# Two gated blocks in float32 on one core: second products of the units issued one half tick later, split inputs and products given more buffers, routing work moved

## The reference, cut to what matters

```python
scores = softmax(xt @ gate_w.T)
_, idx = top_k(scores + gate_bias, 2)
for e in range(8):
    gate_e = sum(where(idx == e, weights, 0.0), axis=1)
    h = silu(xt @ w1[e].T) * (xt @ w3[e].T)
    y = y + gate_e[:, None] * (h @ w2[e].T)
z = silu(xt @ sw1.T) * (xt @ sw3.T) @ sw2.T          # two shared units
return y + z
```

## Time and profile before

| what | value |
|---|---|
| median of three runs | 1388.08 us |
| profiled execution, its own time | 1374.39 us |
| span of its instructions | 1372.6 us |
| TensorE matmuls busy | 1122.3 us (82%) |
| VectorE busy | 1026.4 us (75%) |
| GpSimd busy | 637.2 us (46%) |
| ScalarE busy | 587.4 us (43%) |
| mean granted TensorE clock | 0.92 |

### The profile page before, as it was taken

The page is one execution under the profiler, slowest core; times in us unless marked ns, Lnnn a source line. Parts: engine busy times, 40 slices in busy tenths (PEclk is TensorE's granted clock), DMA queues, the critical chain, the costliest instruction groups (busy, mean ns, idle before and its releaser), DMA issues.

```text
span 1372.6 us, 23593 instructions
## 1 busy us (share of the span) xinstructions
PE 1122.3 (82%) x7464; PEld 961.7 (70%) x7464; DVE 1026.4 (75%) x2393; ACT 587.4 (43%) x1506; POOL 637.2 (46%) x377
## 2 busy tenths in 40 slices
PE   4244446999879996997989999998888888988887
PEld 2133324888768985886878989887777767777776
DVE  2999999989999999985364444447777777777766
ACT  2211212656446553654536454543334443443332
POOL 4889989898789979893301101011111111111000
PEclk9965555999979997999899999999999999999999
DMA  6101114988478965895561555510000000000000
GB/s 214 46 24 38 38 47 155 276 277 255 151 231 281 280 216 171 258 296 180 183 199 53 180 167 184 164 30 21 18 24 24 21 19 24 24 24 24 8 8 16
DMA packets 125036, 166.41 MB, mean 121 GB/s; under 512 B 10033, under 2 KB 67569, under 8 KB 124913
## 3 DMA queue, kind: packets, MB, share of 16 engines
q1 hardware_dynamic: 119792, 152.31, 35.9%
q0 software_dynamic: 5120, 12.59, 2.8%
HBM read 137.60 MB, written 27.26 MB: 120 GB/s over the span
## 4 chain that ended last, share of the span: by engine, by line
PE 55%; DVE 24%; issue 8%; POOL 6%; ACT 3%; SPq 2%; DMA 1%; DVEq 0%; POOLq 0%; ACTq 0%
PE ZB L1274 9%; PE YB L1288 6%; PE YD L1325 4%; DVE q_sb L896 4%; PE ZD L1242 3%; PE ZD L1244 3%; PE ZD L1243 3%; DVE s L871 3%; POOL prod L585 3%; PE ZD L1288 2%; PE YB L1325 2%; DVE hu L1094 2%; PE MC L1238 2%; POOL xs L595 2%; PE MA L1233 2%
## 5 line engine op out<-in xcount | busy, mean ns | idle before, releaser
L561 POOL TENSOR_TENSOR rstd<-ve,neghalf 128x4 f32<-128x4 f32 x64 | 65.7, 1026 | 581.3 <-DVE ve L825 580.9
L682 ACT ACTIVATE hid<-ZB,w2b 128x128 f32<-128x128 f32 x768 | 215.6, 377 | 163.5 <-PE YB L1288 81.5
L573 POOL TENSOR_TENSOR prod<-q_sb,kv_sb 128x2048 f32<-128x2048 f32 x48 | 216.3, 4508 | 53.4 <-DVE q_sb L896 33.3
L585 POOL TENSOR_TENSOR prod<-s,kv_sb 128x2048 f32<-128x2048 f32 x48 | 215.3, 4507 | 7.5 <-DVE q_sb L896 7.5
L1274 PE MATMUL ZB<-bt,w1b 128*128 128x128 f32 x1536 | 212.5, 284 | 1.2 <-ACT hid L682 0.9
L1274 PEld LDWEIGHTS ZB<-bt,w1b 128*128 128x128 f32 x1536 | 196.7, 200 | 4.0 <-issue 3.4
L704 ACT ACTIVATE own_prod<-ZD 128x512 f32<-128x512 f32 x102 | 61.1, 599 | 232.5 <-PE ZD L1244 230.9
L1288 PE MATMUL YB<-w2b,hid 128*128 128x128 f32 x1024 | 141.0, 281 | 0.0
L1288 PEld LDWEIGHTS YB<-w2b,hid 128*128 128x128 f32 x1024 | 128.5, 194 | 14.7 <-ACT hid L682 9.0
L1094 DVE TENSOR_TENSOR hu<-own_prod,ZD 128x512 f32<-128x512 f32 x102 | 69.8, 684 | 72.8 <-ACT own_prod L704 45.4
L1109 DVE SCALAR_TENSOR_TENSOR own_prod<-YD,gate,own_prod 128x128 f32<-128x128 f32 x320 | 89.9, 343 | 30.4 <-PE YD L1325 27.8
(11 more groups left out here) (250 smaller groups left out, 2335.0 us busy)
## 6 DMA issues: line engine op xcount, KB each, us to landing
w2b<-in_w SPq DMA_DIRECT2D x96, 516.0 KB
w1b<-in_w SPq DMA_DIRECT2D x96, 512.0 KB, 4.9
xb<-xs SPq DMA_DIRECT2D x96, 128.0 KB, 3.4
ctx_t<-in_ctx SPq DMA_DIRECT2D x32, 256.0 KB, 2.9
x2d<-x2s SPq DMA_DIRECT2D x48, 128.0 KB, 5.2
x<-in_x SPq DMA_DIRECT2D x16, 256.0 KB, 3.8
xs<-zrow SPq DMA_DIRECT2D x4, 1024.0 KB, 10.6
xrow<-in_x SPq DMA_DIRECT2D x16, 256.0 KB, 3.9
```

The costliest lines, as they stand in the source:

```text
L573: pool.tensor_tensor(out=prod[:, t % 2, :].rearrange("p (h e d) -> p h e d", h=HEADS, e=HEADS), in0=q.unsqueeze(2).broadcast_to([P, HEADS, ...
L585: pool.tensor_tensor(out=prod[:, (t + 1) % 2, :].rearrange("p (h d e) -> p h d e", h=HEADS, e=HEADS), in0=s0[:, t, :, :].unsqueeze(2).broa ...
L682: act.activation(hid[n % 2][:, j, k * RT:(k + 1) * RT], ZB[j // 2][:, at:at + RT], ACT.Relu, bias=w2b[t % 3][:, k, e, FJ * D + j:FJ * D + ...
```

## The change

The second products stand three halves after the first. `hu` gets three buffers, which lie in `prod`, a tile of the attention stage (the weight conversion, which borrowed hu, borrows vk_t and lk_t). ut_hi and ut_lo get two buffers each. The third norm moves half a tick to a tick earlier on GpSimd (kc 7 to kc 6) and a half earlier on ScalarE. ut_lo moves from h15 to h0 on VectorE, the product lg from h0 to h2 on TensorE (behind vk), logits_max from h0 to h3, score_parts from h6 to h5, route_tokens from h4 (behind hu2) to h6. No instruction of computation or transfer is added or taken away.

```diff
-UNIT_OUT = {pos + 2: u for pos, u in UNIT_IN.items()}
+UNIT_OUT = {pos + 3: u for pos, u in UNIT_IN.items()}
@@ bank_uses
-        if not later:
-            order += [(None, "lg", d) for d, k in d_parts(tick) if k == 0]
         stages = C_LATER if later else C_FIRST
         order += [(None, stages[k], c) for c, k in c_parts(tick) if k in stages]
+        if not later:
+            order += [(None, "lg", d) for d, k in d_parts(tick) if k == 1]
@@ buffers
-        ut_hi, ut_lo = sb("ut_hi", [P, CH], F32R), sb("ut_lo", [P, CH], F32R)
-        su, hu = own_prod[:, CH:3 * CH].rearrange("p (i n) -> p i n", i=2), sb("hu", [P, 2, CH])
+        ut_hi, ut_lo = ([sb(f"{n}{i}", [P, CH], F32R)[:] for i in range(2)] for n in ("ut_hi", "ut_lo"))
+        su = own_prod[:, CH:3 * CH].rearrange("p (i n) -> p i n", i=2)
+        hu = [prod[:, 0, i * CH:(i + 1) * CH] for i in range(1, 4)]
-        raw = [hu[:, i, :] for i in range(2)]
+        raw = [vk_t[:], lk_t[:]]
@@ GpSimd
-                        if kc == 7:
+                        if kc == 6:
                             norm(3, c)
@@ ScalarE, first half of a tick
+                        if kc == 7:
+                            if has(c - 1):
+                                filled(act, "xt3", c - 1)
+                            normed(3, lambda j: xn3[:, j, :], lambda j: x3[:, j, :], c)
@@ ScalarE, second half of a tick
                         if kc == 7:
-                            if has(c - 1):
-                                filled(act, "xt3", c - 1)
-                            normed(3, lambda j: xn3[:, j, :], lambda j: x3[:, j, :], c)
                             b = filled(act, "xt3", c)
-                            if has(c - 1):
-                                act.wait_ge(pe_gate.sem, pe_gate.at(c - 1))
-                            act.activation(ut_hi[:], b[:], ACT.Copy).then_inc(ut_hi_s.sem, 1)
+                            if has(c - 2):
+                                act.wait_ge(pe_gate.sem, pe_gate.at(c - 2))
+                            act.activation(ut_hi[c % 2], b[:], ACT.Copy).then_inc(ut_hi_s.sem, 1)
@@ VectorE, unit_gated
-                if u >= 2:
-                    dve.wait_ge(pe_f.sem, pe_f.at(d, max(1, u - 2)))
-                elif has(d - 1):
-                    dve.wait_ge(pe_f.sem, pe_f.at(d - 1, E1 + u))
-                dve.tensor_tensor(out=hu[:, u % 2, :], ...
+                old = d * UNITS + u - 3
+                if old >= 0:
+                    dve.wait_ge(pe_f.sem, pe_f.at(old // UNITS, max(1, old % UNITS)))
+                dve.tensor_tensor(out=hu[(d * UNITS + u) % 3], ...
@@ VectorE, first half of a tick
                         if kd == 0:
-                            logits_max(d)
+                            dve.wait_ge(ut_hi_s.sem, ut_hi_s.at(d))
+                            b = filled(dve, "xt3", d)
+                            dve.tensor_tensor(out=ut_lo[d % 2], in0=b[:], in1=ut_hi[d % 2].bitcast(F32), op=ALU.subtract).then_inc(free_of("xt3", d), 1)
...
-                        if kc == 3:
-                            score_parts(c)
                     for d, kd in d_parts(tick):
                         unit_half(d, 2 * kd)
-                        if kd == 2:
+                        if kd == 3:
                             route_tokens(d)
@@ VectorE, second half of a tick
+                    for d, kd in d_parts(tick):
+                        if kd == 1:
+                            logits_max(d)
                     for c, kc in c_parts(tick):
                         if kc == 1:
                             score_max(c)
+                        if kc == 2:
+                            score_parts(c)
...
-                        if kc == 7:
-                            dve.wait_ge(ut_hi_s.sem, ut_hi_s.at(c))
-                            b = filled(dve, "xt3", c)
-                            dve.tensor_tensor(out=ut_lo[:], in0=b[:], in1=ut_hi[:].bitcast(F32), op=ALU.subtract).then_inc(free_of("xt3", c), 1)
@@ TensorE, unit_in
                 pair, earlier = PAIR[d, u]
+                emptied(pe, "xt3", d)
@@ TensorE, the loop
-                if not later:
-                    for d, kd in d_parts(tick):
-                        if kd == 0:
-                            cross("lg", d)
                 stages = C_LATER if later else C_FIRST
                 for c, kc in c_parts(tick):
                     if kc in stages:
                         cross(stages[kc], c)
+                if not later:
+                    for d, kd in d_parts(tick):
+                        if kd == 1:
+                            cross("lg", d)
```

More of the change, by code:

```diff
@@ L702, in unit_silu @@
                 if d * UNITS + u >= 2:
-                    act.wait_ge(hu_s.sem, hu_s.at(d, u - 1))
+                    act.wait_ge(hu_s.sem, d * UNITS + u - 1)
                 act.activation(su[:, u % 2, :], unit_pair[PAIR[d, u][0]][0][:], ACT.Silu).then_inc(silu_s.sem, 1)
@@ L1089, in unit_gated @@
                 dve.wait_ge(pe_gate.sem, pe_gate.at(d, u + 1))
-                if u >= 2:
-                    dve.wait_ge(pe_f.sem, pe_f.at(d, max(1, u - 2)))
-                elif has(d - 1):
-                    dve.wait_ge(pe_f.sem, pe_f.at(d - 1, E1 + u))
-                dve.tensor_tensor(out=hu[:, u % 2, :], in0=su[:, u % 2, :], in1=unit_pair[PAIR[d, u][0]][1][:], op=ALU.mult).then_inc(hu_s.sem, 1)
+                old = d * UNITS + u - 3
+                if old >= 0:
+                    dve.wait_ge(pe_f.sem, pe_f.at(old // UNITS, max(1, old % UNITS)))
+                dve.tensor_tensor(out=hu[(d * UNITS + u) % 3], in0=su[:, u % 2, :], in1=unit_pair[PAIR[d, u][0]][1][:], op=ALU.mult).then_inc(hu_s.sem, 1)
             def unit_sum(d, u):
@@ L1304, in unit_in @@
                     ns = slice((2 * u + i) * P, (2 * u + i + 1) * P)
-                    three(unit_pair[pair][i][:], w13_hi[:, ns], w13_lo[:, ns], ut_hi[:], ut_lo[:]).then_inc(done.sem, 1)
+                    three(unit_pair[pair][i][:], w13_hi[:, ns], w13_lo[:, ns], ut_hi[d % 2], ut_lo[d % 2]).then_inc(done.sem, 1)
             def unit_out(d, u):
@@ L1322, in unit_out @@
                         for v in range(SHARED):
-                            last = pe.matmul(b[:, js], hu[:, v, js], w2u_sb[:, v, :], start=(v == 0), stop=(v == SHARED - 1))
+                            last = pe.matmul(b[:, js], hu[(d * UNITS + v) % 3][:, js], w2u_sb[:, v, :], start=(v == 0), stop=(v == SHARED - 1))
                     else:
-                        last = pe.matmul(b[:, js], hu[:, u % 2, js], w2u_sb[:, u, :], start=True, stop=True)
+                        last = pe.matmul(b[:, js], hu[(d * UNITS + u) % 3][:, js], w2u_sb[:, u, :], start=True, stop=True)
                 last.then_inc(pe_f.sem, 1)
@@ L1382, in cross @@
                         cols = slice(2 * j * E1, 2 * (j + 1) * E1)
-                        pe.matmul(b[:, cols], ut_hi[:, js], wg_parts[:], start=True, stop=False)
-                        last = pe.matmul(b[:, cols], ut_lo[:, js], wg_high[:], start=False, stop=True)
+                        pe.matmul(b[:, cols], ut_hi[c % 2][:, js], wg_parts[:], start=True, stop=False)
+                        last = pe.matmul(b[:, cols], ut_lo[c % 2][:, js], wg_high[:], start=False, stop=True)
                     last.then_inc(done, 1)
```

## The result

The changed kernel takes **1306.05 us** (median of four runs, 1301.73 to 1309.39) against 1387.36 us before (four runs, three of them those of the 1388.08 above); the ratio is 0.9408, 95% interval 0.938 to 0.9435. Its profiled execution took 1305.32 us, with a span of 1303.6 us.

A forecast was written before the change was run, and what follows sets the result against it. A once-per-period loop through VectorE, TensorE and ScalarE, 32.9 us, was taken to set the period, replacing 37.7. Terms -4 - 4 - 47 - 1.6 - 2.5 = -59 took 1388.1 to 1329 us, range 1314 to 1352.

The forecast's parts named there:

- The old waits: TensorE's idle time before out3, out7, xt3 and lg, 5.59 us a period together; forecast gone, out7's within 0.1 us.
- What is late next: New TensorE waits in a period: 0.65 us before xt2, 0.65 before vv, and out4 waiting for hu4.
- The loop: Chain hu2, hu4, out4, xt3, xt2, in1, hu2, once round per period: 32.9 us, taken as 33.0, setting the period.
- TensorE's floor: TensorE's own work in a period without waits: 31.6 us.
- The median of the runs stood 13.7 above it; I keep that: Timed median assumed to stay 13.7 us above the profiled execution: 1315 us profiled, 1329 us median.
- The clock gives more: Rival: clock dips, 1.6 us each, vanish with the 2.53 us wait; median 1316 us or so; chance 0.14.
- the floor case: Period at TensorE's floor, giving the same 1316 us or so as the clock rival.
- the ten periods: Sixth chunk's xt3 to the sixteenth's: 10 x -4.7 = -47 us, plus -1.6 for a half-speed stretch.
- the part before 917 us: Attention untouched, full expert stretches 0, gain only between two expert blocks at 698 to 728: -4 us, ends 0 and -6.
- the last chunk: From its xt3 to the end of the span, 35.8 us: -2.5 us, ends 0 and -4.
- The longer loop by ScalarE's change of table: Rival: unseen waits, such as the table change before silu2, give a period of 34 to 35.3, 1340 to 1353 us; chance 0.20.
- The slower end: Rival: VectorE's present idle time stays unused, period 40.9 us, +32, 1420 us; chance 0.05.

The follow-up runs named there:

- e3: Changed kernel with the third norm put back (GpSimd at kc 7, ScalarE's normed behind silu9): 1329.0 us, ratio 0.9575 to the old kernel.
- e10: Changed kernel with ut_lo, lg and logits_max back at h15, h0 and h0: 1343.7 us, ratio 0.9673 to the old kernel.
- e4: Changed kernel with logits_max moved in front of hu1 on VectorE and out9 in front of xt2 on TensorE: 1296.8 us, ratio 0.9345 to the old kernel.
- e7: Changed kernel with two hu buffers instead of three: 1319.54 us, ratio 0.9509 to the old kernel.
- e9: Old kernel with 8 extra overwritten products (16 matmul instructions) issued in the wait before out3, from chunk 5 on: 1376.75 us, ratio 0.9915.
- e1: Old kernel run again, unchanged: 1387.97 us, ratio 0.9999; profiled execution 1383.87 us.
- before: The old kernel, without the change: 1387.36 us.
- fillers: Old kernel with extra overwritten products in the wait before out3: sixteen products 1385.35 us, eight products 1376.75 us.
- after: The changed kernel: 1306.05 us, ratio 0.9408 to the old kernel.
- e6: Changed kernel with one buffer each for ut_hi and ut_lo: 1307.89 us, ratio 0.9422 to the old kernel.
- e11: Changed kernel run again, unchanged: 1306.47 us, ratio 0.9409 to the old kernel.
- e2: Old kernel with only route_tokens moved, from behind hu2 to behind hu3: 1389.36 us, ratio 1.0008.
- e8: Changed kernel with second products two halves behind as before and routing behind hu3, all other moves kept: 1353.16 us, ratio 0.9758 to the old kernel.

## Why the prediction was right in its steps and wrong in its number

**The old waits** went as told, all four, and at the places where the walk put them. e3 and e10 show the price of two of them: 1.8 us a period for the one before xt3; 1.3 for the one before lg, clock aside (33.6 against 32.3: the wait is 2.18, but the 0.56 and the 0.35 go).

**What is late next**: three places were named, before xt2, before vv and before out4, and they are the three of the profile, none over 1 us. Their size was too large: 0.65, 0.65 and next to nothing forecast, 0.56, 0.35 and under 0.1 found.

**The loop** of 32.9 us can be read off the rows after. xt3 to xt2 took 2.91 (forecast 2.94), xt2 to in1 4.43 (4.5), in1 to hu2 6.43 (6.5), hu2 to hu4 7.76 (7.8), hu4 to out4 0.83 (0.84). The last leg, out4 to the next xt3, is 10.1 against 10.3 (its own terms, five of 0.88 and four of 1.5, add up to 10.4): I had taken 0.88 for an out-product, the value behind a wait, where one in a full stream takes 0.81. That is 32.46 for this one period; the other nine are 32.32 to 32.35. TensorE's floor is 31.37 (e4) where I had 31.6. I had 32.9 from the loop and 31.6 + 0.65 + 0.65, also 32.9, from floor plus waits: they lie so close together that both describe the period, and the number alone doesn't decide between them. e7 speaks for the loop: hu2 starts 14.40 us after xt3 there, not 13.77, a new wait of 0.54 stands before out4, and the period grows by 0.8.

**The step that failed first** is the sentence on the median, "The median of the runs stood 13.7 above it; I keep that". The surplus was, for the most part, not a constant beside the kernel: it was the clock, falling in or just behind the 2.53 us wait that the change takes away. e9 takes 11.1 us off the old kernel by filling that wait and nothing else; less the one dip that the table has already, that is about 9.5 of the 12.3 that are missing. After the change the median stands 0.7 above the profiled execution, not 13.7. The rival "The clock gives more" named this mechanism (1316 us, still 10 above what was measured, for the three terms below), and I gave it 0.14, with the argument that nine periods of the profile had the wait and no dip. One execution is one draw: e1's profile has five dips in ten periods. And the range never put that rival together with terms that come out larger: its lower end, 1314, was the clock case or the floor case, each alone. The two numbers that were on the table, a profile with one dip and three timed runs all 12 to 17 us above it, should have weighed more than the nine periods.

**Three terms were sized too small**, 10 us in all: the ten periods (55.0 against 48.6, from the waits and the out-product above), the part before 917 us (6.8 against 4) and the last chunk (3.7 against 2.5). For the early part, profiles of before and of its fillers reach the fifth xt3 at 918.8, 920.5, 922.2 and 923.5 us and after at 912.0, 913.9, and e6 at 915.7. So the gain there is nearer 7 than 4. The traces show where it lies. Of the 6.4 us of waits that I had named between 698 and 728, 1.5 stay (0.95 and 0.53 before two outs) and 4.9 go, where I took 4. Another 1.5 comes from the full expert stretches, for which the forecast has "so 0": from the fourth chunk's xt3 to the fifth's takes 64.56 to 64.61 us in the four profiles of before and of its fillers and 63.05 to 63.08 in after, e4, e6 and e11. In before, the fifth xt3 waits 0.92 us for xn3, and in after it doesn't; with the third norm put back (e3) it waits 1.10 and the distance is 64.36. The rows that I had read, 765 to 820, hold no such wait. The clock also differed between 670 and 700 (0.83 in before, 0.94 in e1 and in after), so part of the distance between single profiles is chance.

**The rivals.** The longer loop by ScalarE's change of table did not come: silu2 starts 1.30 after the change's start. The rule of the Trainium skill (ScalarE: Activation LUTs, What ACT_TABLE_LOAD costs) with its drain would give 2.66; the trace doesn't agree. The slower end did not come either; VectorE's idle time shrank from 10.3 to 6.0 us a period (26.35 of 32.35 busy).

**Which parts carry it.** The third norm's move 23 us, the move of ut_lo, lg and logits_max 37 (half of it dips, by e10's profile), the distance of three with the routing's half 47, the third hu buffer 13, the second ut buffers nothing that can be measured. They overlap and don't add up to 81, since each was taken away from a schedule in which the others stay.

## What to carry to other kernels

Walk a periodic schedule once round, queue by queue, with start-to-start distances from rows; it gave this one's waits within 0.3 us and its period within 2%. A large wait is worth moving only together with whatever next stands in the same queue: e2 moved the routing alone and moved a 2.5 us wait into a 2.2 us one. Where timed runs stand above a profiled one, look at the granted clock behind TensorE's longest waits (2.1 to 2.5 us here) in more than one profile before calling the difference an offset; a few products that nobody reads, in such a wait, are a cheap test (e9), and a cheap gain where the wait cannot go.

## What the runs showed of the hardware that I had not expected

- TensorE's granted clock falls in waits of 2.1 to 2.5 us or up to 1.4 us behind them, in some periods and not in others of the same execution: in 1 and 5 of 10 in the two profiles of before, 1 in e2's, 8 in e10's. A dip costs 1.5 to 1.7 us, and twice that in four of e10's periods. With waits of 1.61 us or less none came in 10 periods each of after (twice), e3, e4, e6, e7 and e8; but in e10's last chunk one began 0.5 us behind a wait of 1.50, so no length of wait is shown to be safe. What decides between a dip and none, and why e10 has so many more than e2 behind waits of the same length, is not shown. The Trainium skill (TensorE: Matmul & The Clock Gate, Part 1) has the slow clock as the default that activity lifts, and the runs agree: added work kept it at 1.00.
- A kernel that issues 16 more matmul instructions a period, all overwritten, runs 0.85% faster (0.9902 to 0.9929).
- At a full TensorE, 313.70 of 313.70 us, weight loads are busy for 271.36, 87%, in this mix of float32 and float32r products.
